# Attention outputs of all batches normalised by VectorE in two wide chunks from gathered denominators

## What is computed

```python
attn_w = softmax(einsum('bhqd,bhkd->bhqk', q, k) * scale)
attn_out = einsum('bhqk,bhkd->bhqd', attn_w, v)          # self
x = x + gate_a * (attn_out @ W_proj + b_proj)
c_attn_w = softmax(einsum('bhqd,bhsd->bhqs', q_c, k_c) * scale)
x = x + (c_attn_w @ v_c) @ W_cproj + b_cproj             # cross
x = x + gate_m * (gelu(x_norm2 @ W_mlp1 + b_mlp1) @ W_mlp2 + b_mlp2)
```

## Time and profile before

| | |
|---|---|
| median of 2 runs | 1496.12 us (1495.04 to 1497.2) |
| profiled execution, own time | 1498.68 us |
| its span, first to last instruction | 1496.5 us |
| mean granted TensorE clock | 0.976 |
| busy: TensorE, VectorE, ScalarE, GpSimd | 1379.4, 1111.4, 1094.9, 708.3 us |

### The profile page before, as it was taken

The page is one execution under the profiler, slowest core; times in us unless marked ns, Lnnn a source line. Parts: engine busy times, 40 slices in busy tenths (PEclk is TensorE's granted clock), DMA queues, the critical chain, the costliest instruction groups (busy, mean ns, idle before and its releaser), DMA issues.

```text
span 1496.5 us, 39974 instructions
## 1 busy us (share of the span) xinstructions
PE 1379.4 (92%) x15090; PEld 908.1 (61%) x15090; DVE 1111.4 (74%) x1992; ACT 1094.9 (73%) x1852; POOL 708.3 (47%) x995
## 2 busy tenths in 40 slices
PE   3567899999999999999999999999999999999877
PEld 1334566666666666666666666666666666665545
DVE  4647877788777777787777787887777777875535
ACT  3145787777788887777788887787788877877653
POOL 2233344455545544555545544555455544555421
PEclk8689999999999999999999999999999999999989
DMA  5122233333332333333333233333332333332111
GB/s 178 45 78 87 88 95 95 96 109 98 98 93 94 94 95 99 99 109 96 94 96 94 91 99 99 100 108 93 92 99 90 97 95 96 109 95 68 59 32 35
DMA packets 142132, 137.97 MB, mean 92 GB/s; under 512 B 38069, under 2 KB 116566, under 8 KB 141942
## 3 DMA queue, kind: packets, MB, share of 16 engines
q1 hardware_dynamic: 141942, 135.42, 29.1%
HBM read 56.34 MB, written 9.55 MB: 44 GB/s over the span
## 4 chain that ended last, share of the span: by engine, by line
PE 70%; DVE 10%; DMA 8%; issue 3%; ACT 3%; POOL 3%; SPq 2%; DVEq 0%; ACTq 0%; POOLq 0%
PE dense_ps L348 14%; PE dense_ps L349 12%; PE dense_ps L350 12%; PE o_ps L696 11%; PE max_ps L661 10%; PE exp_ps L678 6%; DMA o_rb_cross<-r_dram_cross 4%; DVE mx_cross L1015 4%; PE dense_ps L596 4%; DVE mx_self L1015 2%; DMA r_dram_cross<-o_r_cross 2%; ACT probs L818 1%; SPq L433 1%; POOL o_n_cross L1150 1%; POOL Y L1179 1%
## 5 line engine op out<-in xcount | busy, mean ns | idle before, releaser
L818 ACT ACTIVATE probs<-exp_ps 128x1024 f32<-128x1024 f32 x512 | 525.9, 1027 | 185.7 <-PE exp_ps L678 183.2
L1015 DVE TENSOR_REDUCE mx_cross<-max_ps 128x4 f32<-128x1024 f32 x256 | 313.3, 1224 | 100.2 <-PE max_ps L661 92.4
L1015 DVE TENSOR_REDUCE mx_self<-max_ps 128x4 f32<-128x1024 f32 x256 | 312.3, 1220 | 75.8 <-PE max_ps L661 73.4
L1150 POOL TENSOR_TENSOR o_n_self<-o_n_self,o_rb_self 128x512 f32<-128x512 f32 x32 | 40.6, 1269 | 295.9 <-DMA o_rb_self<-r_dram_self 295.9
L1183 POOL TENSOR_TENSOR g_split<-G,g_split 128x512 f16<-128x512 f32 x120 | 136.7, 1161 | 58.1 <-ACT g_split L807 58.1
L348 PE MATMUL dense_ps<-xt,mlp_hi 128*128 128x256 f16 x512 | 139.8, 273 | 3.0 <-DVE xt L979 2.8
L348 PE MATMUL dense_ps<-mlp_hi,g_split 128*128 128x256 f16 x504 | 139.6, 277 | 1.1 <-DVE g_split L1093 1.1
L350 PE MATMUL dense_ps<-xt,mlp_lo 128*128 128x256 f16 x512 | 139.6, 273 | 0.0
L349 PE MATMUL dense_ps<-xt,mlp_hi 128*128 128x256 f16 x512 | 139.5, 273 | 0.0
L350 PE MATMUL dense_ps<-mlp_hi,g_split 128*128 128x256 f16 x504 | 138.9, 276 | 0.0
L349 PE MATMUL dense_ps<-mlp_lo,g_split 128*128 128x256 f16 x504 | 138.9, 276 | 0.0
(11 more groups left out here) (230 smaller groups left out, 3338.0 us busy)
## 6 DMA issues: line engine op xcount, KB each, us to landing
q_stack_self<-split_q SPq DMA_DIRECT2D x192, 64.0 KB, 2.6
k_stack_self<-split_k SPq DMA_DIRECT2D x192, 64.0 KB, 2.6
k_stack_cross<-split_kc SPq DMA_DIRECT2D x192, 64.0 KB, 2.6
q_stack_cross<-split_qc SPq DMA_DIRECT2D x192, 64.0 KB, 2.6
X<-in_x SPq DMA_DIRECT2D x32, 256.0 KB, 2.8
Ctx<-in_ctx SPq DMA_DIRECT2D x32, 256.0 KB, 3.3
rows_a<-rows_a_dram SPq DMA_DIRECT2D x32, 256.0 KB, 3.3
o_n_self<-o_sb_self SPq DMA_DIRECT2D x64, 128.0 KB, 2.8
```

Of the source, the lines that this page charges most:

```text
L818: nc.scalar.activation(probs[:, t % 8:t % 8 + 2], exp_ps[:], ACT.Exp).then_inc(exp_taken[kind], 2)
L1015: nc.vector.tensor_reduce(mx[kind][:, :, :, t // 2].rearrange("p q a -> p a q"), max_ps[:].rearrange("p a (q k) -> p a q k", q=2), AX_X, A ...
L1150: nc.gpsimd.tensor_tensor(o_n[kind][:], o_n[kind][:], o_rb[kind][:], ALU.mult).then_inc(o_mult[kind], 1)
```

## The change

All batches and kinds go the way that the last cross batch went. SP issues eight gathers instead of six transfers: for each chunk c of 256 columns two of denominators into `o_rb` and two of outputs into `o_n`, 64 partitions each. The chunks are done at two steps: chunk 0 where the small reciprocal stood (`o_recip`), chunk 1 where the subtraction stood (`o_lo`). The steps `r_out`, `r_back`, `o_norm` and `o_hi` are gone, with `r_dram`, `o_d` and `o_r`; `o_gather` waits for `ot_lo` of the batch before, and TensorE's `proj` and `cproj` wait for both chunks. `PLAN` and `AHEAD` lose the entries of the dropped steps; for the last batch `AHEAD` gets `o_lo_cross: 15`, so that its two chunks stand in adjacent slots.

```diff
-    "o_gather_self": (1, 0, 11), "o_recip_self": (1, 0, 12), "r_out_self": (1, 0, 15), "r_back_self": (1, 1, 1),
-    "o_norm_self": (1, 1, 1), "o_hi_self": (1, 1, 3), "o_lo_self": (1, 1, 4), "rows_a": (0, 1, 1),
+    "o_gather_self": (1, 0, 11), "o_recip_self": (1, 0, 12),  "o_lo_self": (1, 1, 4), "rows_a": (0, 1, 1),
...
-            def o_gather_last(b, kind):
-
-                sp_wait(ot_lo[kind], b.n)
-                sp_wait(o_mult[kind], b.n)
+            def o_gather(b, kind):
+
+                sp_wait(ot_lo[kind], b.n * 2)
                 for c in range(C):
                     sp_wait(o_copied[kind], b.n * 4 + 2 * c + 2)
                     for g in range(2):
                         nc.sync.dma_start(o_rb[kind][64 * g:64 * g + 64, c], o_sb[kind][1:P:2, g, c * T:(c + 1) * T]
-                                          ).then_inc((o_d_in, o_n_in)[c][kind][b.u], 16)
+                                          ).then_inc(o_in[c][kind][b.u], 16)
                         nc.sync.dma_start(o_n[kind][64 * g:64 * g + 64, c], o_sb[kind][0:P:2, g, c * T:(c + 1) * T]
-                                          ).then_inc((o_d_in, o_n_in)[c][kind][b.u], 16)
-
-            def o_gather(b, kind):
...
-            def r_store(b, kind):
...
-            def r_fetch(b, kind):
...
                 if (b := due("cproj")):
-                    pe.wait_ge(ot_lo["cross"], b.n + 1)
+                    pe.wait_ge(ot_lo["cross"], b.n * 2 + 2)
...
-                for kind in KINDS:
-                    if (b := due(f"o_hi_{kind}")) and not (kind == "cross" and b.n == LAST):
-                        act.wait_ge(o_mult[kind], b.n + 1)
-                        wait_count(act, ready["proj" if kind == "self" else "cproj"], b.n)
-                        nc.scalar.activation(ot[kind][:, 0], o_n[kind][:], ACT.Copy).then_inc(ot_hi[kind], 1)
...
                 for kind in KINDS:
-                    if (b := due(f"o_recip_{kind}")) and kind == "cross" and b.n == LAST:
-                        dve.wait_ge(ready["cproj"], b.n)
-                        for c in range(C):
-                            dve.wait_ge((o_d_in, o_n_in)[c][kind][b.u], b.pair * 16 * (c + 1) + 16 * 4)
+                    for c in range(C):
+                        if (b := due((f"o_recip_{kind}", f"o_lo_{kind}")[c])):
+                            dve.wait_ge(ready["proj" if kind == "self" else "cproj"], b.n)
+                            dve.wait_ge(o_in[c][kind][b.u], dmas(b, 4))
                             then(nc.vector.reciprocal(o_rb[kind][:, c], o_rb[kind][:, c]))
                             then(nc.vector.tensor_tensor(o_n[kind][:, c], o_n[kind][:, c], o_rb[kind][:, c], ALU.mult))
                             then(nc.vector.tensor_copy(ot[kind][:, 0, c], o_n[kind][:, c]))
-                            last = nc.vector.tensor_tensor(ot[kind][:, 1, c], o_n[kind][:, c], ot[kind][:, 0, c], ALU.subtract)
-                        last.then_inc(ot_lo[kind], 1)
-                    elif b:
-                        dve.wait_ge(o_d_in[kind][b.u], dmas(b, 1))
-                        wait_dmas_before(dve, r_out[kind], b, 1)
-                        nc.vector.reciprocal(o_r[kind][:], o_d[kind][:]).then_inc(o_recip[kind], 1)
-                    if (b := due(f"o_lo_{kind}")) and not (kind == "cross" and b.n == LAST):
-                        dve.wait_ge(ot_hi[kind], b.n + 1)
-                        nc.vector.tensor_tensor(ot[kind][:, 1], o_n[kind][:], ot[kind][:, 0], ALU.subtract
-                                                ).then_inc(ot_lo[kind], 1)
+                            nc.vector.tensor_tensor(ot[kind][:, 1, c], o_n[kind][:, c], ot[kind][:, 0, c], ALU.subtract
+                                                    ).then_inc(ot_lo[kind], 1)
...
-                    if (b := due(f"o_norm_{kind}")) and not (kind == "cross" and b.n == LAST):
-                        pool.wait_ge(o_n_in[kind][b.u], dmas(b, 2))
-                        pool.wait_ge(o_rb_in[kind][b.u], dmas(b, 2))
-                        nc.gpsimd.tensor_tensor(o_n[kind][:], o_n[kind][:], o_rb[kind][:], ALU.mult).then_inc(o_mult[kind], 1)
```

More of the change, by code:

```diff
@@ L221, in block_kernel @@
         o_n = {k: sb(f"o_n_{k}", [P, C, T]) for k in KINDS}
-        o_d = {k: sb(f"o_d_{k}", [P, 32]) for k in KINDS}
-        o_r = {k: sb(f"o_r_{k}", [P, 32]) for k in KINDS}
         o_rb = {k: sb(f"o_rb_{k}", [P, C, T]) for k in KINDS}
@@ L246, in block_kernel @@
         o_copied = {k: sem(f"o_copied_{k}") for k in KINDS}
-        o_recip = {k: sem(f"o_recip_{k}") for k in KINDS}
-        o_mult = {k: sem(f"o_mult_{k}") for k in KINDS}
-        ot_hi, ot_lo = ({k: sem(f"{n}_{k}") for k in KINDS} for n in ("ot_hi", "ot_lo"))
+        ot_lo = {k: sem(f"ot_lo_{k}") for k in KINDS}
         stats_done, mv_done = ({k: sem(f"{n}_{k}") for k in LN} for n in ("stats", "mv"))
@@ L261, in block_kernel @@
         mrow_in = {k: sems(f"mrow_{k}") for k in KINDS}
-        o_n_in, o_d_in, r_out, o_rb_in = (
-            {k: sems(f"{n}_{k}") for k in KINDS} for n in ("o_n_in", "o_d_in", "r_out", "o_rb_in"))
+        o_in = [{k: sems(f"o_in_{c}_{k}") for k in KINDS} for c in range(2)]
         bias_in = sem("bias_in")
@@ L510, in at @@
                     if (b := due(f"o_gather_{kind}")):
-                        (o_gather_last if kind == "cross" and b.n == LAST else o_gather)(b, kind)
-                    if (b := due(f"r_out_{kind}")) and not (kind == "cross" and b.n == LAST):
-                        r_store(b, kind)
-                    if (b := due(f"r_back_{kind}")) and not (kind == "cross" and b.n == LAST):
-                        r_fetch(b, kind)
+                        o_gather(b, kind)
                 if (b := due("store")):
@@ L734, in at @@
                 if (b := due("proj")):
-                    pe.wait_ge(ot_lo["self"], b.n + 1)
+                    pe.wait_ge(ot_lo["self"], b.n * 2 + 2)
                     tokens_out(b, "proj", ot["self"], "proj", 0)
```

30 lines of the change are left out of this document (5 added, 25 removed), and 4 rows, old and new, of the table AHEAD.

## The result

| | before | after |
|---|---|---|
| median of 2 runs | 1496.12 us | 1910.85 us (1902.75 to 1918.94) |
| ratio, 95% interval | | 1.2768 [1.2671, 1.2866] |
| profiled execution: own time, span | 1498.68, 1496.5 us | 1918.94, 1917.2 us |
| mean granted TensorE clock | 0.976 | 0.903 |

A forecast was written before the change was run, and what follows sets the result against it. TensorE was taken as full, VectorE's free fifth as unusable. To 1498.68 us came 289 of stalls (10.7 a period x 27) and 46 of clock falls: 1834, so about 1831 us against the median; range 1725 to 1905.

The forecast's parts named there:

- the four places named: VectorE's four chunk positions in a period, A, B, C and D, forecast to add 8.86 us together before gather waits.
- B: First self chunk on VectorE: takes 2.92 us instead of 0.46, adding 2.46 us a period, with no slack worth the name.
- C: Second self chunk on VectorE: takes 2.92 us instead of 0.67, adding 2.25 us a period; TensorE's proj waits directly for it.
- D: First cross chunk on VectorE: 2.65 us more, less 0.35 idle ahead of the next reduction, so 2.30 us a period.
- A: Second cross chunk on VectorE: 2.32 us more, less 0.47 idle ahead of a reduction, so 1.85 us a period; cproj waits too.
- ramp and tail: 9 of the 63 sets of two chunks, outside the steady part: bounds -41 and +48 us, taken 0.
- the number of clock falls: TensorE's clock drops after new gaps: none to three a period, one of 1.71 us taken, 46 us over 27 periods.
- a relief worth zero: Multiply removed from GpSimd for each batch and kind: at most TensorE's 0.2 us a period could come back, taken as zero.
- The gather waits: VectorE waiting for SP's transfers at both first chunks: 0.65 us (self) and 1.2 (cross), 1.85 a period; bounds 0 and 4.1.
- The rival with three falls: TensorE's clock falls at every gap, three a period, giving 1923 us; chance 0.04 for a time over 1905.
- Its high end: Top of the forecast range, 1905 us: 1.6 more clock falls a period than the one taken, adding 74 us.
- The estimate of 2.13 us: Reciprocal of 256 columns on VectorE at 8 cycles an element and 0.96 GHz; set aside for the measured 1.74 us.

## Why the prediction was wrong, step by step

**What was right.** The mechanism: VectorE had no use for its free fifth, TensorE stalls at the four places named, the wide reciprocal is the price, and it has the forecast length (1745 ns for self, 1743 for cross). VectorE's 45.33 us of a period and TensorE's 45.54 were forecast as 43 and 42 of 54. TensorE's idle time, 289 us in the sum, measured 277. That nearness is partly luck: two errors cancel in it, as the places show (us a period; the waits of the long stretch of after, less the 8.4 us for `mx_cross`, 2.5 for `mx_self` and 2.1 for `xn` in the stretch of before, over 28):

| place | forecast with gather wait | measured |
|---|---|---|
| B, first self chunk | 2.46 + 0.65 | 2.07 |
| C, second self chunk | 2.25 | 4.06 |
| D and A, cross chunks | 2.30 + 1.2 + 1.85 | 3.17 |
| behind A, through GpSimd's queue | none | 0.78 |

**Where the miss lies.** The sum was 1834 us for this execution, which took 1919. In the sum's own terms the stalls came out 12 us smaller (277 for 289), the loss by the clock 58 larger (104 for 46), ramp and tail 39 larger (39 for 0). So two steps failed in size, the number of clock falls and the ramp and tail that were put at nothing; and within the stalls one cost was missing, at C.

**C: a step that was missing.** The prediction gave every chunk the 2.92 us of the earlier trace rows, from the one place in the trace of before where GpSimd stood idle beside it, and took GpSimd's part as a relief worth zero. That a VectorE instruction could be longer because of what GpSimd does at that moment was in no term and no rival. It cost 53 us of VectorE's time and 71 us in all; with GpSimd's part moved the kernel takes 1848 us, which is inside the range. The trace of before had one warning: the subtraction of 128x512 that takes 0.68 us in the earlier trace rows took 1.07 where it stood beside a GpSimd addition (VectorE's row, then GpSimd's, of before):

```profile
1451.83 1.07 DVE L1037 TENSOR_TENSOR ot_cross<-o_n_cross,ot_cross 128x512 f16<-128x512 f32 x1 [1.74 <-ACT ot_cross L831]
```

```profile
1451.10 1.26 POOL L1179 TENSOR_TENSOR Y<-Y,X 128x512 f32<-128x512 f32 x1
```

In the period shown of before, the subtraction at C ends at 723.81 and GpSimd's three low parts begin at 724.34; the chunk that takes its place is 2.25 us longer and reaches into them.

**The gather waits: too large.** 1.85 us a period were taken, 0.24 measured (6.7 / 28), all of it at B. The transfers land 2.0 us after their issue, not 2.7, which takes 0.7 us off at each of the two places:

```profile
o_rb_self<-o_sb_self SPq DMA_DIRECT2D x128, 64.0 KB, 2.0
```

The error at C (1.81 us a period too little) and the one at the gathers (1.61 too much) nearly cancel, and that is luck. They have no common root: with C at its plain length the wait at D stays small (4.7 us in the whole execution), because SP comes earlier too, 11.1 us after the `mt_self` copy instead of 12.9. Its `k_stack_self` transfers stand ahead of the gather and need the split of `k`, which VectorE makes behind C. Only where VectorE comes earlier against SP does the wait at D come: without a self chunk at C (99 and 57 us, more than was feared), beside the idle matmuls (24) and with the narrow reciprocal (16).

**The clock: right in kind and in the size of a fall (1.7 us), wrong in number.** One fall a period was taken, and there are 60 in 28 periods: TensorE works 3.73 us longer a period, 104 us in 28, or 1.7 a fall, where 46 stood in the sum. The prediction read a mean clock of 0.95 from the ramp of before and set it against its count of gaps; the steady part has 0.92. The rival with three falls, 1923 us, at a chance of 0.04, comes nearest to the time, but by luck: it has 138 us of clock loss and nothing in ramp and tail. The gap behind C is the one that the prediction held too short for a fall; with GpSimd held off it has nearly the forecast length, 2.3 us, and brings a fall in 19 of 28 periods all the same.

**Ramp and tail: taken as zero, 39 us.** 28 and not 27 periods have the steady price, so 7 sets of chunks remain: 5.6 us each, against 13.64 / 2 = 6.8 in the steady part. Outside the long stretch TensorE's busy time grew by 13.6 us (1379.4 - 1163.64 to 1497.4 - 1268.08) with as many matmuls, which is clock; the other 25 us are waiting. So the removed trip through DRAM gave back little or nothing there; why was not tried, and this part of the miss stays open.

**The range.** Its high end had 289 us of stalls and 120 us of clock (46 and 74 more), both above what was measured. What put the time over it are the 39 us of ramp and tail. For these the prediction itself gave bounds, -41 and +48, but the high end did not take them in.

**The reciprocal's length.** The estimate of 2.13 us from the Trainium skill, page "VectorE: DVE Perf Modes", section "First, the fixed hardware budget", is not borne out: 1745 and 1743 ns are measured, as the row of before had it.

## What to carry over

Before an instruction is moved or widened on VectorE, look not only at what waits for it but at what GpSimd does in the same microseconds, in both orders: a chain of short dependent instructions can take its length from the GpSimd instructions beside it. The cost of a transfer that is issued late belongs to the pair (when it lands, when its reader comes): repairing another stall can bring it out, so it is tested together with that stall. Where an almost full TensorE gets new stalls, do not count falls of the clock for the longest alone: here a stall of 4.2 us had one in every period, and stalls of about 2 us in half of them or more. And every term that has bounds goes into the range with them, also one whose likeliest value is zero.

## What the runs showed of the hardware

VectorE beside GpSimd: 128x256 product 0.43 to 0.65 us, copy to float16 0.29 to 1.13, subtraction 0.43 to 1.26, each of the long ones ending 0.16 to 0.28 us after a GpSimd instruction, while GpSimd's own took 1.15 to 1.33 each. The reciprocal was not slowed: 1.74 us in the first chunk of cross, with GpSimd's `XR` addition (813.87 to 815.13) beside it, and 1.74 at C, with the first low part beside its last 0.74 us. The Trainium skill, page "SBUF — State Buffer", section "SBUF: two separate sides", says that VectorE and GpSimd share a pair of SBUF ports that one instruction holds to its end while the other waits, and that VectorE takes it for an instruction with two SBUF inputs or in a two-port mode. The order of the ends at C agrees with such a lock. That the copy, with one input, runs in a two-port mode is something that no run here shows by itself.

What a fall of the clock costs hangs on what else is late: the idle matmuls, which take away the fall behind C, brought 22 us alone and, with an earlier transfer that by itself gives nothing, 63.
